# Group 1's values by seven block products, with the sums of M moved to VectorE and the closing stores on two queues

## The reference

```python
h = jnp.maximum(_layernorm(x, axis=-1), 0.0)           # x: (64, 128, 512)
output = einsum('bni,io->bno', h, weight)               # values, weight 512x512
q, k = einsum('bni,io->bno', h, wq), einsum('bni,io->bno', h, wk)
alpha = maximum(einsum('bno,bmo->bnm', q, k), 0.0) * (adj != 0)
alpha = softmax(alpha, axis=1)
x = x + einsum('bnm,bmo->bno', alpha, output)
```

## Time and profile before

| | before |
|---|---|
| median of three executions | 415.41 us |
| the profiled execution: time / span | 415.38 us / 413.5 us |
| TensorE busy | 405.9 us, 98% of the span |
| VectorE busy | 297.0 us, 72% |
| ScalarE busy | 277.7 us, 67% |
| GpSimd busy | 264.7 us, 64% |

### The profile page before, as it was taken

How to read it: one execution, slowest core, us unless ns; L and a number is a source line. 1 busy time by engine, 2 the same in 40 slices (tenths; PEclk the granted TensorE clock), 3 DMA queues, 4 the chain that set the end, 5 groups by cost and what they waited for, 6 DMA issues and landing times.

```text
span 413.5 us, 9484 instructions
## 1 busy us (share of the span) xinstructions
PE 405.9 (98%) x3581; PEld 322.1 (78%) x3581; DVE 297.0 (72%) x569; ACT 277.7 (67%) x590; POOL 264.7 (64%) x284
## 2 busy tenths in 40 slices
PE   8999999999999999999999999999999999999995
PEld 5444545879798897979798797979889797979883
DVE  5799789596767777676767777676777667656465
ACT  4749877576767677776776776776867777643534
POOL 0749896969395875849486775939577584910003
PEclk9999999999999999999999999999999999999999
DMA  8973868978969797896979598796988699393022
GB/s 290 370 102 72 208 112 222 251 169 198 196 195 195 226 151 211 201 217 171 180 237 180 134 235 210 195 208 179 187 248 162 159 213 236 41 186 103 2 103 101
DMA packets 161641, 75.03 MB, mean 181 GB/s; under 512 B 135360, under 2 KB 143808, under 8 KB 161600
## 3 DMA queue, kind: packets, MB, share of 16 engines
q1 hardware_dynamic: 161312, 73.94, 77.9%
q10 hardware_dynamic: 288, 0.52, 0.3%
HBM read 24.12 MB, written 16.78 MB: 99 GB/s over the span
## 4 chain that ended last, share of the span: by engine, by line
PE 78%; DVE 7%; POOL 6%; ACT 6%; issue 2%; DVEq 0%; ACTq 0%
PE bank L1136 10%; PE bank L1139 10%; PE bank L1138 10%; PE bank L1153 9%; PE bank L1154 9%; PE bank L1151 9%; PE s_bank L1167 3%; PE s_bank L1166 3%; PE s_bank L1165 3%; PE bank L1172 2%; PE bank L1174 2%; PE bank L1173 2%; POOL hn_lo L423 2%; ACT h L543 2%; DVE raw_stats L828 1%
## 5 line engine op out<-in xcount | busy, mean ns | idle before, releaser
L423 POOL TENSOR_TENSOR hn_lo<-h,hn_hi 128x512 f16<-128x512 f32 x64 | 74.6, 1177 | 51.3 <-ACT hn_hi L553 51.2
L543 ACT ACTIVATE h<-x_sb,shift,rstd 128x512 f32<-128x512 f32 x64 | 49.9, 803 | 21.8 <-POOL shift L418 21.8
L449 POOL TENSOR_TENSOR hn_lo<-s,hn_hi 128x512 f16<-128x512 f32 x56 | 63.1, 1160 | 0.3 <-ACT hn_hi L558 0.3
L1138 PE MATMUL bank<-hT_lo,mt_hi 128*128 128x256 f16 x224 | 61.1, 273 | 0.0
L1136 PE MATMUL bank<-hT_hi,mt_hi 128*128 128x256 f16 x224 | 61.1, 273 | 0.0
L1139 PE MATMUL bank<-hT_hi,mt_lo 128*128 128x256 f16 x224 | 61.1, 273 | 0.0
L1153 PE MATMUL bank<-wt_lo,hT_hi 128*128 128x256 f16 x224 | 61.1, 273 | 0.0
L1151 PE MATMUL bank<-wt_hi,hT_hi 128*128 128x256 f16 x224 | 61.1, 273 | 0.0
L1154 PE MATMUL bank<-wt_hi,hT_lo 128*128 128x256 f16 x224 | 61.1, 273 | 0.0
L558 ACT ACTIVATE hn_hi<-s 128x512 f16<-128x512 f32 x56 | 33.7, 625 | 28.0 <-POOL s L438 23.1
L1136 PE MATMUL bank<-hT_hi,m_hi 128*128 128x256 f16 x168 | 45.8, 273 | 0.9 <-ACT bank L580 0.9
(11 more groups left out here) (166 smaller groups left out, 1104.7 us busy)
## 6 DMA issues: line engine op xcount, KB each, us to landing
out_h<-x_sb SPq DMA_DIRECT2D x63, 256.0 KB, 2.1
x_sb<-in_x SPq DMA_DIRECT2D x15, 1024.0 KB, 5.6
adj_sb<-in_adj SPq DMA_DIRECT2D x16, 256.0 KB, 5.4
hn_hi<-in_L_gnn_wq SPq DMA_DIRECT2D x4, 256.0 KB, 5.5
x_sb<-in_x SPq DMA_DIRECT2D x2, 512.0 KB, 7.1
w_sb<-in_L_gnn_weight SPq DMA_DIRECT2D x2, 512.0 KB, 8.7
hn_lo<-in_L_gnn_wk ACTq DMA_DIRECT2D x2, 256.0 KB, 4.0
hn_lo<-in_L_gnn_wk SPq DMA_DIRECT2D x2, 256.0 KB, 3.8
```

Source lines behind the costliest of these rows:

```text
L423: nc.gpsimd.tensor_tensor(hn_lo[:, s, b], h[:, b], hn_hi[:, s, b], ALU.subtract).then_inc(h_split, 1)
L449: nc.gpsimd.tensor_tensor(low, s32[:, f], high, ALU.subtract).then_inc(s_split, 1)
L543: nc.scalar.activation(h[:, b], x_sb[:, s, b], ACT.Relu, bias=shift[:, b:b + 1], scale=rstd[:, b:b + 1]).then_inc(h_made, 1)
L1138: nc.tensor.matmul(o, bh[:, k, cols], al[:, :, k], start=False, stop=False, skip_group_check=True)
```

## The change

- Group 1's values are made by the seven products (FIRST_V = 1). It now needs its sums of h: POOL makes them (`sums_of_h(1, 1)`, `lows_of_sums(1, 1)`) ahead of group 2's, ACT makes their high parts, SP transposes them (`transpose_sums(1)`, ahead of the load of x of group 3). Banks of groups 0 and 1 are dealt out anew, and ACT's copies and DVE's sums and low parts for group 1 are written into the order by hand.
- M's four sums go from POOL to DVE, ahead of `softmax_shift(0)`.
- W's four sums on POOL follow each other without the scales of group 1 between.
- In group 2's period two `hi_of_sum` of group 3 go behind `copy_p1_v` and `copy_p5_v`.
- P5's copies and the C22 sums use `w_sb` as buffer, and mt32 gets a buffer of its own.
- The last group's stores: graph 0 and the first half of graph 3 are issued by ACT, the other three by SP.

```diff
@@ SP
+                if g == FIRST_V + 2:
+                    sp.wait_ge(v_filled, made_v(g - 2, N_P4))
...
             load_adj(3)
+            transpose_sums(1)
             sp.wait_ge(mt_summed, 4)
             load_x(3)
...
-            for b in (1, 0, 2):
-                if b == 0:
-                    sp.wait_ge(last_added, 1)
-                else:
-                    sp.wait_ge(out_read, GB * LAST + b)
+            for b in (1, 2):
+                sp.wait_ge(out_read, GB * LAST + b)
                 sp.dma_start(out_dram[:, GB * LAST + b:GB * LAST + b + 1, :],
...
-            for f in range(2):
-                sp.wait_ge(out_read, B - 1 + f)
...
+            sp.wait_ge(out_read, B)
+            sp.dma_start(out_dram[:, B - 1, HD:], x_sb[:, LAST % UNROLL, GB - 1, HD:]).then_inc(stored[LAST % UNROLL], 16)
@@ POOL
-            for b in range(GB):
-                lo_of_h(1, 1, b)
-            pool.wait_ge(m_copied, K)
-            nc.gpsimd.tensor_tensor(mt32[:, T1], m32[:, 0:HK, HD:], m32[:, 0:HK, :HD], ALU.subtract).then_inc(mt_summed, 1)
...
+            layernorm_scales(1)
+            sums_of_h(1, 1)
             layernorm_scales(2)
-            pool.wait_ge(mt_summed, 3)
-            nc.gpsimd.tensor_tensor(mt32[:, T4], m32[:, HK:, :HD], mt32[:, T2], ALU.subtract).then_inc(mt_summed, 1)
-            lo_of_h(2, 0, 0)
...
+            lows_of_sums(1, 1)
+            pool.wait_ge(s_split, sums(2, 0))
+            sums_of_h(2, 0)
             lows_of_sums(2, 0)
             layernorm_scales(3)
@@ ACT
             hi_of_sum(2, 0, 2, S2)
             hi_of_sum(2, 0, 3, S4)
-            hi_of_whole_v(1, 0)
+            copy_p1_v(1)
+            hi_of_v11(1)
             normalise_h(3, 3, 0)
+            copy_p5_v(1)
             hi_of_h(3, 1, 0, turn(0, 1))
...
+            hi_of_v22(1)
+            hi_of_v12(1)
+            hi_of_v21(1)
             hi_of_sum(3, 1, 0, S1)
             hi_of_sum(3, 1, 1, S3)
-            hi_of_sum(3, 1, 2, S2)
-            hi_of_sum(3, 1, 3, S4)
             period(0, FIRST)
@@ DVE
             lo_of_whole_t(0, 3)
+            vec.wait_ge(m_copied, K)
+            nc.vector.tensor_tensor(mt32[:, T1], m32[:, 0:HK, HD:], m32[:, 0:HK, :HD], ALU.subtract).then_inc(mt_summed, 1)
...
             softmax_shift(0, 0, 1)
+            lo_of_whole_v(0, 3)
...
+            lo_of_wt(3)
+            lo_of_v(1, 0, bank[VA][:], 0, 0)
+            sum_x_v(1)
+            lo_of_mt(0)
+            lo_of_mt(1)
             make_mask(2, 0, 2)
             lo_of_mt(2)
+            sum_c22_v(1)
             lo_of_mt(3)
+            lo_of_v(1, 1, c22_v, 1, 1)
+            lo_of_v(1, 2, bank[VE][:], 0, 1)
+            lo_of_v(1, 3, bank[VB][:], 1, 0)
@@ PE
+            product_v(1, N_P1, bank[VA][:], True)
             pe.wait_ge(p_split, GB)
...
+            pe.wait_ge(v_copied, done_v(1, 1))
+            product_v(1, N_P2, bank[VA][:], False)
+            pe.wait_ge(sT_landed[1], 2 * 16)
+            pe.wait_ge(wt_split, T1 + 1)
+            pe.wait_ge(out_read, HG)
+            product_v(1, N_P5, bank[VE][:], True)
+            pe.wait_ge(wt_split, T2 + 1)
+            product_v(1, N_P6, bank[VB][:], False)
+            scores(1, 1, quadrants=False)
+            pe.wait_ge(v_summed, done_v(1, 1))
+            pe.wait_ge(wt_split, T3 + 1)
+            product_v(1, N_P7, bank[VB][:], False)
+            product_v(1, N_P3, bank[VE][:], False)
+            pe.wait_ge(v_summed, done_v(1, 2))
+            pe.wait_ge(wt_split, T4 + 1)
+            product_v(1, N_P4, bank[VB][:], False)
             pe.wait_ge(out_read, GB)
             for g in range(FIRST, LAST):
                 period(g // UNROLL, g % UNROLL)
```

More of the change, by code:

```diff
@@ L63, in made_v, with done_v @@
     def made_v(g, n):
+        if isinstance(g, int) and g == FIRST_V and n in (N_P2, N_P5):
+            n = N_P2 + N_P5 - n
         if isinstance(g, int) and g == LAST and n in (N_P2, N_P6):
             n = N_P2 + N_P6 - n
-        return made(g, n)
+        return 7 * g + (n - 7 * FIRST_V)
     def done(g, n):
         return 2 * g + (n - 2 * FIRST)
+    def done_v(g, n):
+        return 2 * g + (n - 2 * FIRST_V)
     def sums(g, n):
-        return 4 * g + (n - 4 * FIRST)
+        return 4 * g + (n - 4 * FIRST_V)
     def whole(g, n):
@@ L110, in graph_attention_kernel @@
         v_lo = sb("v_lo", [N, GB, D], F16)
-        spare = sb("spare", [N, 4, HG, HD], F32)
         last_out, last_p32 = s32[:, 0].rearrange("p a b -> p (a b)"), s32[:, 1].rearrange("p a (b n) -> p (a b) n", n=N)
-        p5_t, p5_v, c22_t, c22_v = (spare[:, k].rearrange("p a b -> p (a b)") for k in range(4))
         w_sb = sb("w_sb", [N, K, D], F32)
+        p5_t, p5_v, c22_t, c22_v = (w_sb[:, k] for k in range(4))
         wt32 = sb("wt32", [N, 4, HK, HD], F32)
@@ L537, in normalise_h @@
                 act.wait_ge(rstd_made, 1 if isinstance(g, int) and g == 0 and b < HG else g + 2)
[L538 removed]
+                if isinstance(g, int) and g <= FIRST_V:
                     if g > 0:
@@ L550, in hi_of_h @@
                     act.wait_ge(hT_landed[s], 2 * 16 * turns)
-                if b == 0 and not (isinstance(sum_turns, int) and sum_turns == 0):
-                    act.wait_ge(sT_landed[s], 2 * 16 * sum_turns)
+                    act.wait_ge(sT_landed[s], 2 * 16 * turns)
                 nc.scalar.activation(hn_hi[:, s, b], h[:, b], ACT.Copy).then_inc(h_hi_made, 1)
@@ L675, in period @@
                 copy_p1_v(g)
+                if isinstance(g, int) and g == FIRST:
+                    hi_of_sum(3, 1, 2, S2)
                 copy_p5_v(g)
+                if isinstance(g, int) and g == FIRST:
+                    hi_of_sum(3, 1, 3, S4)
                 hi_of_p(g - 1)
@@ L1058, in _ @@
             stats_all(3, 3, 0)
+            lo_of_whole_t(1, 2)
             stats_all(3, 3, 1)
-            lo_of_whole_t(1, 2)
+            lo_of_whole_t(1, 3)
+            residual(0, 0, 0)
+            residual(0, 0, 1)
             stats_all(3, 3, 2)
             stats_all(3, 3, 3)
-            lo_of_whole_t(1, 3)
-            for b in range(GB):
-                residual(0, 0, b)
-            make_mask(2, 0, 2)
-            lo_of_mt(0)
-            lo_of_whole_v(1, 0)
-            lo_of_mt(1)
-            lo_of_whole_v(1, 1)
-            lo_of_wt(3)
-            lo_of_whole_v(1, 2)
+            residual(0, 0, 2)
+            residual(0, 0, 3)
+            lo_of_wt(3)
[3 more added lines that the diff above has]
+            lo_of_mt(1)
+            make_mask(2, 0, 2)
             lo_of_mt(2)
-            lo_of_whole_v(1, 3)
+            sum_c22_v(1)
             lo_of_mt(3)
+            lo_of_v(1, 1, c22_v, 1, 1)
+            lo_of_v(1, 2, bank[VE][:], 0, 1)
+            lo_of_v(1, 3, bank[VB][:], 1, 0)
             period(0, FIRST)
@@ L1286, in whole_product_t @@
                 for k in range(K):
-                    nc.tensor.matmul(M_BANK[c], m_hi[:, k, cols], hT_hi[:, s, 0:GB, k], start=k == 0, stop=False)
-                    nc.tensor.matmul(M_BANK[c], m_hi[:, k, cols], hT_lo[:, s, 0:GB, k], start=False, stop=False)
-                    last = nc.tensor.matmul(M_BANK[c], m_lo[:, k, cols], hT_hi[:, s, 0:GB, k], start=False,
+                    nc.tensor.matmul(t_bank(g)[c], m_hi[:, k, cols], hT_hi[:, s, 0:GB, k], start=k == 0, stop=False)
+                    nc.tensor.matmul(t_bank(g)[c], m_hi[:, k, cols], hT_lo[:, s, 0:GB, k], start=False, stop=False)
+                    last = nc.tensor.matmul(t_bank(g)[c], m_lo[:, k, cols], hT_hi[:, s, 0:GB, k], start=False,
                                             stop=k == K - 1)
```

118 lines of the change are left out of this document (53 added, 65 removed).

## The result

| | before | after |
|---|---|---|
| median of five executions | 415.41 us | 419.93 us (419.56 to 420.81) |
| the profiled execution: time / span | 415.38 / 413.5 us | 420.81 / 419.0 us |
| TensorE busy | 405.9 us, 98% | 405.0 us, 97% |

The ratio of the times is 1.0109, with a 95% interval of 1.0097 to 1.0122: slower by 1.1%, 4.5 us in the medians. The forecast was 418.6 us, the range 415.0 to 420.6. The median lies in the range, 1.3 us above the forecast.

The account below looks back on a forecast made before the run. TensorE, busy 98% of the span, was taken to bound the kernel. 415.38 + 3.8 (group 2's outputs late: 5.5 lost, 1.7 back) - 0.55 (last store) = 418.6 us, range 415.0 to 420.6.

Parts of the forecast that it names:

- S4 of group 2 ends: GpSimd's list up to group 2's last sum: ends near 62.5 us (bounds 61 to 63.5), before at 57.70.
- P7: Product of group 1's values on TensorE: waits for sum_x behind group 3's scales and normalisation, starts at 71.8 us.
- wait before P4: TensorE idle from 74.4 us for 3.5 us, waiting for sum_c22 behind VectorE's mask and M's low parts.
- group 2's period starts: TensorE, end of P4: at 79.3 us and not at 73.81, so 5.5 us late.
- The nothing for W's sums: W's four sums in one go on GpSimd, ahead of group 1's low parts: gain 0.
- Its softmax is as late as TensorE, not later: Group 2's period: softmax adds no delay, waits of 1.07, 0.26 and 0.37 go, 1.7 us back, outputs 3.8 us late.
- 0.55 us saved: The end: last store issued near 410.37 us instead of 410.92, landing 2.2 us either way.
- the fast rival: GpSimd's added 9.6 us are hidden and all gains come: 411.7 us, or 413 with half the waits; chance 0.1.
- Three holds of 0.55: M's sums on VectorE: sharing with GpSimd delays GpSimd's list by three holds of 0.55 us, 1.65 in the sum.
- the first rival: Values little late: P4's waits 1.9 us or less, M's sums slip between GpSimd's scale instructions; 415.3 to 417.2 us, chance 0.2.
- The rival of the clock: Clock falls to 1.2 GHz in TensorE's new gap of 3.5 to 4.7 us: +1.3 to +2.6, near 420.5; chance 0.07.
- The rival of SyncE's queue: Group 3's x lands 1 to 2 us later than 61, behind group 1's transposes: 419.6 to 420.6 us; chance 0.08.

Follow-up runs that it names:

- wsums_alone: The kernel before with W's four sums in a row on GpSimd, ahead of group 1's scales: 415.30 us, ratio 0.9998.
- copies_alone: The kernel before with only the new order of ScalarE's high parts in group 2's period: 414.18 us, ratio 0.9970.
- stores_alone: The kernel before with only the last stores issued on two queues: 415.31 us, ratio 1.0000.
- no_low_sums: The kernel after with only four elements of each low part of group 1's sums made on GpSimd, high parts transposed in their place: 419.96 us, ratio 1.0107.
- msums_on_gpsimd: The kernel after with M's four sums back on GpSimd behind group 1's sums: 423.3 us, ratio 1.0191.
- c22_first_filled: c22_first with 16 useless matmuls in TensorE's wait before group 1's outputs: 417.56 us, ratio 1.0056.
- c22_first: The kernel after with VectorE's sum_c22 ahead of the mask and M's last two low parts: 419.2 us median, ratio 1.0091; profiled execution 417.63 us.
- msums_on_gpsimd_filled: msums_on_gpsimd with useless matmuls (24 and 22) in TensorE's two long waits: 423.82 us, ratio 1.0207.
- copies_and_msums: The kernel before with the new order of group 2's copies and M's four sums on VectorE together: 413.3 us, ratio 0.9951.

## Why the prediction came out as it did

**Right.** The direction, and the chain that makes the loss, stage by stage:

| | forecast | after | after, less 0.55 of late loads |
|---|---|---|---|
| S4 of group 2 ends | 62.5 | 62.8 | 62.2 |
| P2 of V starts | 63.9 | 63.98 | 63.4 |
| P5 | 65.9 | 66.06 | 65.5 |
| P7 | 71.8 | 71.99 | 71.4 |
| wait before P4 | 3.5 | 2.88 | 2.88 |
| group 2's period starts | 79.3 | 78.99 | 78.4 |

The last column is the one to judge by: the dates are 0.3 to 0.5 early up to P7. Part of that is in the forecast's own sums: 60.5 + 5.2 is 65.7 where it has 65.9, and 69.7 + 0.7 + 0.65 + 0.6 is 71.65 where it has 71.8. That the raw dates agree within 0.3 is luck of the loads. The nothing for W's sums (wsums_alone) was right too. The profiled execution carries 0.55 us of late loads, so of the 5.2 us by which group 2's period is late 4.6 are the change's: the 5.5 of the forecast was 0.9 too much. Some 0.6 of that stands in the wait before P4, the forecast's largest term: VectorE's run from M's low parts to the end of sum_c22 took from 71.85 to 77.6, 5.8 us, where 2.2 + 3.3 + 0.6 = 6.1 were forecast, and P7 and P3 ended at 74.8 and not at 74.4. The contended waits in this run are 5.8 - 2.8 = 3.0 us, so taking the probabilities' row for it (3.3) was the right choice. M's rows would have given even less than the 1.9 of the forecast: the trace of before has a fourth such low part, at 70.64, which took 0.68, so the four together waited 1.4.

**Wrong: "Its softmax is as late as TensorE, not later".** The forecast gave 1.7 us back in group 2's period (alone, copies_alone kept 1.2 of them); 73.81 to 88.62 was 14.81 us before and would have become 13.1. It is 94.06 - 78.99 = 15.07, 2.0 more. The waits for the copies went, but between the end of P4 (78.99) and group 1's outputs TensorE has only eight products, 10.6 us. In the same time VectorE finishes the values' low parts and starts the shift at 81.4, its small `shift_max` takes 1.06 beside GpSimd, the exponentials start at 83.90, and the low parts of the probabilities end at 90.9: 11.9 us. In between VectorE does two statistics and the mask of 1.40 (0.43 in before), and starts the low parts at 89.15. ScalarE meanwhile does three copies and the two high parts that the change moved there; the first high part of the probabilities is ready near 88.7, before VectorE is free, so the two moved ones are not what the low parts wait for. The forecast looked at the shift alone and never added up the chain behind it. Its own rows held a warning: in before the low parts end at 84.35 + 1.11 = 85.46 and the outputs start at 85.66, so time taken away ahead of the outputs is gained only if the softmax comes earlier by as much. The outputs then start 1.4 late and are held up for 0.5 by a residual, where the forecast had the old 0.37 vanish. Together: 3.8 - 0.9 + 2.0 = 4.9. The 0.9 too much hides part of the 2.0 and 0.55 too little, so it is in part luck that the total comes as near as it does.

**Wrong: the end.** "0.55 us saved" was 0.0 (stores_alone). The earlier issue is real, but landing then took 2.7 to 2.9 us in place of 2.2. The forecast named this as the condition ("nothing if the other queue's landing is slower by that much"), and took the lack of a row against it for a row in its favour. The sum as it came: 415.38 + 4.9 + 0.55 of loads = 420.8, which the profiled execution took.

**Partly wrong: what S4 of group 2 decides.** The forecast had two chains to P7: GpSimd's to S4 and its low parts (67.0), and VectorE's through the probabilities, the residuals and the statistics (67.5). no_low_sums bears the second out: with S4 at 59.76 GpSimd waits for the statistics and P7 comes only 0.4 us earlier. So the sign that the fast rival (chance 0.1) was to be told by, S4 ended by 60.4 and nothing late, is wrong: there S4 ended by then, and P5, P7 and P4 were late. Both chains run behind group 1's four sums on GpSimd, which stand ahead of the scales of group 2 in its list; msums_on_gpsimd, which puts these scales back by 3.1 us more, costs 3.4.

**Partly wrong: the price of M's sums.** "Three holds of 0.55" were assumed. In after three sums took 0.68 and one 1.54. They slipped in between GpSimd's small instructions for the scales of group 2, and held two of these up by 0.3 each (0.47 and 0.53 us for 0.20 in the earlier trace rows): that half of the first rival was right. S4 still ended at 62.8, and one thing that the forecast did not have is that two of W's low parts were held up more (3.56 us against 2.43 in the earlier trace rows). T's last low parts stand behind them on VectorE and came 1.7 us later (44.72 against 43.05, 0.55 of it the loads'), which made the unforeseen wait of 0.68 before the scores at 46.05.

**The rival of the clock** (chance 0.07) did not come true in the profiled execution of after: its wait of 2.88 us was followed by matmuls at full speed (P4 took 1.32). In three of the four timed ones the mean clock of 0.993 to 0.996 says that it probably fell, but the time did not rise to show for it. The mechanism is real: it was seen in no_low_sums and msums_on_gpsimd, and c22_first_filled prices it at 1.6 us in c22_first.

**The rival of SyncE's queue** (chance 0.08): x of group 3 was issued at 54.5 and landed after 7.2 us, near 61.7, and VectorE's statistics waited 0.23 us for it. That is the forecast's 61 with the loads' 0.55, so this rival did not come true.

**Open.** Three of after's four timed executions ran at a mean granted clock of 0.993 to 0.996 and took 419.56 to 420.27 us, the one at 0.998 took 419.93; by msums_on_gpsimd_filled a slow stretch can lie in the shadow of other waits, but that was not tried on after itself. Nor was a fuller rearrangement of VectorE's list, with which group 1's seven products might yet earn some of their 1.15 us; the best of the tried ones (417.56, with matmuls of no use in it) is 4.3 us behind copies_and_msums.
